# Where the joins, the softmax probabilities and each layer's last scoring stand in a graph network kernel

## What is computed

```python
def _gat_layer(x, src, dst, W_i, a_src_i, a_dst_i, b_i):
    h = (x @ W_i).reshape(n, H, C)
    es = jnp.einsum('nhc,hc->nh', h, a_src_i)
    ed = jnp.einsum('nhc,hc->nh', h, a_dst_i)
    e = es[src] + ed[dst]
    e = jnp.where(e > 0, e, NEG_SLOPE * e)
    m = jax.ops.segment_max(e, dst, num_segments=n)
    p = jnp.exp(e - m[dst])
    denom = jax.ops.segment_sum(p, dst, num_segments=n)
    alpha = p / denom[dst]
    msg = alpha[:, :, None] * h[src]
    out = jax.ops.segment_sum(msg, dst, num_segments=n)
    return out.reshape(n, H * C) + b_i
...
out1 = jax.ops.segment_sum(edge_attr, col, num_segments=n)
mx = jax.ops.segment_max(edge_attr, col, num_segments=n)
```

## Time and profile before

| | us |
|---|---|
| median of three runs | 9205.75 |
| lowest and highest of them | 9204.99 and 9205.83 |
| the profiled execution | 9206.7 |
| its span, first to last instruction | 9204.5 |

### The profile page before, as it was taken

How to read it: one execution, slowest core, us unless ns; L and a number is a source line. 1 busy time by engine, 2 the same in 40 slices (tenths; PEclk the granted TensorE clock), 3 DMA queues, 4 the chain that set the end, 5 groups by cost and what they waited for, 6 DMA issues and landing times.

```text
span 9204.5 us, 130223 instructions
## 1 busy us (share of the span) xinstructions
PE 5638.7 (61%) x34288; PEld 4521.8 (49%) x34288; DVE 5424.6 (59%) x12708; ACT 4487.3 (49%) x8146; POOL 5326.3 (58%) x5192
## 2 busy tenths in 40 slices
PE   4999879974555555555455555555534545455456
PEld 3777646653454544444445445444434444444444
DVE  6888721134666666666466666666645555555555
ACT  3555400024655555554455565555525555555554
POOL 2000100047777777775677777777757777777770
PEclk9999989965555555555555555555555555555558
DMA  3333335504444444443344444444423333333331
GB/s 102 136 140 140 126 140 188 181 9 124 113 123 116 118 121 114 124 113 89 88 120 116 123 113 122 117 116 122 103 66 80 84 82 86 80 86 81 86 80 32
DMA packets 601478, 989.12 MB, mean 107 GB/s; under 512 B 331106, under 2 KB 455043, under 8 KB 561523
## 3 DMA queue, kind: packets, MB, share of 16 engines
q0 software_dynamic: 163760, 357.05, 17.9%
q1 hardware_dynamic: 217540, 544.34, 16.9%
q10 hardware_dynamic: 219648, 81.82, 3.4%
HBM read 758.42 MB, written 224.34 MB: 107 GB/s over the span
## 4 chain that ended last, share of the span: by engine, by line
PE 27%; DVE 21%; DVEq 17%; POOL 16%; issue 13%; DMA 5%; ACT 1%; POOLq 0%; SPq 0%; ACTq 0%
POOL arena L650 14%; DVEq L1281 14%; PE bank L976 13%; DVE acc L1879 10%; DMA arena<-row_table,staged_idx 4%; PE bank L1199 3%; PE bank L1001 3%; DVE arena L1835 2%; PE bank L1139 2%; DVEq L1879 2%; DVE arena L1866 2%; DVE x_mem L1553 1%; DVE arena L1828 1%; PE bank L1264 1%; DVEq L1871 1%
## 5 line engine op out<-in xcount | busy, mean ns | idle before, releaser
L650 POOL DMA_INDIRECT arena<-row_table,staged_idx x4992 | 5039.4, 1009 | 1624.7 <-issue 1504.0
L1199 PE MATMUL bank<-arena 128*128 128x136 f32 x9984 | 2486.6, 429 | 1004.4 <-DVE acc L1879 843.5
L1199 PEld LDWEIGHTS bank<-arena 128*128 128x128 f32 x9984 | 2194.0, 315 | 1169.3 <-issue 1163.3
L1879 DVE TENSOR_TENSOR acc<-acc,bank 128x136 f32 x4992 | 1477.2, 296 | 1020.1 <-issue 796.5
L805 ACT ACTIVATE pick_dist<-col,dst_local 128x128 bf16<-128x128 f32 x4992 | 1518.5, 387 | 59.2 <-PE bank L1199 58.5
L976 PE MATMUL bank<-arena 128*128 128x385 bf16 (+1 forms) x7546 | 1342.2, 327 | 49.5 <-DVE arena L1657 33.0
L598 POOL TENSOR_TENSOR arena<-acc,node_stat 128x896 f32 x14 | 24.4, 1744 | 1729.1 <-POOLq L610 955.2
L1155 PE MATMUL bank<-ident,arena 128*32 128x128 f32 x624 | 161.5, 414 | 1347.3 <-DVE arena L1798 1347.3
L976 PEld LDWEIGHTS bank<-arena 128*128 128x128 bf16 x7546 | 711.1, 98 | 476.1 <-DVE arena L1657 33.2
L1795 DVE TENSOR_TENSOR arena<-arena 128x128 f32<-128x128 f32 x156 | 60.8, 390 | 1381.7 <-DMA arena<-row_table,staged_idx 1381.7
L1866 DVE TENSOR_TENSOR arena<-arena,prob 128x528 f32<-128x528 f32 x1248 | 837.3, 691 | 0.5
(11 more groups left out here) (356 smaller groups left out, 5676.2 us busy)
## 6 DMA issues: line engine op xcount, KB each, us to landing
arena<-dst_rows SPq DMA_DIRECT2D x156, 1024.0 KB, 5.8
cell_rows<-arena SPq DMA_DIRECT2D x76, 1568.0 KB, 5.2
arena<-cell_rows SPq DMA_DIRECT2D x76, 1568.0 KB, 6.5
arena<-row_table,staged_idx POOLq DMA_INDIRECT x4992
edge_stats<-x_mem ACTq DMA_DIRECT2D x416, 192.0 KB, 3.9
x_mem<-in_edge_attr SPq DMA_DIRECT2D x208, 192.0 KB
x_mem<-segment_flags SPq DMA_DIRECT2D x416, 96.0 KB
arena<-change_rows SPq DMA_DIRECT2D x312, 64.0 KB
```

What stands on the lines that cost most here:

```text
L650: pool.indirect_dma_start(gathered[:, at, :], None, table, bass.IndirectOffsetOnAxis(staged_idx[:, at:at + 1], 0)).then_inc(att_gathered[n ...
L1199: mm = pe.matmul(region(k)[:, 0:ROW], pick[:, k, :], gathered[:, b * GROUP + k, :], start=True, stop=True)
L1879: done = dve.tensor_tensor(row, row, region(m * BATCH + k), ALU.add)
```

## The change

Three things change.

1. In layer three alone (`n` of 2), `prob` is no longer the SBUF tensor but the first 128 columns of PSUM bank 0 or 1, by the group's parity (`prob_of`). ACT's exponential writes there, and `weigh` reads it from there.
2. `join_streams` is cut in two. `take_carry` (one copy out of bank 0) stays in front of layer three. The seven joins are written out and stand behind the adds of the groups 26 to 32 of that layer, one each; the first has the wait for the gathered statistics.
3. In group 50 of each layer (`head` and not `ahead`) the head of group 51 isn't woven in any more: DVE and PE do it behind all eight batches, ACT does its two exponentials behind its last picks (in layers one and two behind the copies of the statistics too).

```diff
+        JOIN_FROM = NG // 2
+        def prob_of(n, b):
+            if n < STATS_LAYERS:
+                return prob[:, b, :, :]
+            return bank[:, b, 0:HEADS * GROUP].rearrange("p (h s) -> p h s", h=HEADS)
...
-                    nc.scalar.activation(prob[:, b, :, :], score[:, :, :], ACT.Exp).then_inc(att.prob, 1)
+                    nc.scalar.activation(prob_of(n, b), score[:, :, :], ACT.Exp).then_inc(att.prob, 1)
...
-                            if head:
+                            if head and ahead:
                                 act_exps(n * NG + g + 1, 1 - b)
...
                     if n < STATS_LAYERS:
                         scan_out(n, g, 1)
+                    if head and not ahead:
+                        act_exps(n * NG + g + 1, 1 - b)
...
+                    between = head and ahead
                     for m in range(NBATCH):
                         sum_batch(G, b, m)
-                        if head and m == 2:
+                        if between and m == 2:
                             turn_scores(G + 1)
...
+                    if head and not between:
+                        turn_scores(G + 1)
+                        turn_ends(G + 1)
+                        turn_crossings(G + 1)
+                        turn_maxima(G + 1)
                     if head:
                         spread_scale(G + 1)
...
-            def join_streams():
+            def take_carry():
                 dve.wait_ge(st.carry_spread, 1)
                 dve.tensor_copy(carry_row[:, :], bank[:, 0, 0:2 * EA])
-                dve.wait_ge(n3.stats_gathered, 16 * NT)
-                then()
+                then()
+
+            def join_streams(i):
...
+                if i == 0:
+                    dve.wait_ge(n3.stats_gathered, 16 * NT)
+                    dve.sem_inc(dve_tick, 1)
...
-                                      prob[:, b, :, m * BATCH:(m + 1) * BATCH].rearrange("p h s -> p s h").unsqueeze(3)
+                                      prob_of(n, b)[:, :, m * BATCH:(m + 1) * BATCH].rearrange("p h s -> p s h").unsqueeze(3)
...
+                    if head and not between:
+                        score_edges(G + 1, 1 - b, use)
+                        first_scans(G + 1, 1 - b, use)
+                        carries(G + 1, 1 - b)
+                        last_scans(G + 1, 1 - b)
+                        shift_scores(G + 1, 1 - b, slot + GROUP)
+                    if n == STATS_LAYERS and JOIN_FROM <= g < JOIN_FROM + NTG:
+                        join_streams(g - JOIN_FROM)
 
                 if n == STATS_LAYERS:
-                    join_streams()
+                    take_carry()
                 score_edges(n * NG, 0, 0)
```

More of the change, by code:

```diff
@@ L1206, in pe_group @@
                     slot = it * (2 * GROUP) + (b + 2) * GROUP
+                    between = head and ahead
                     for m in range(NBATCH):
                         sum_batch(G, b, m)
-                        if head and m == 2:
+                        if between and m == 2:
                             turn_scores(G + 1)
-                        if head and m == 3:
+                        if between and m == 3:
                             turn_ends(G + 1)
-                        if head and m == 4:
+                        if between and m == 4:
                             turn_crossings(G + 1)
-                        if head and m == 5:
+                        if between and m == 5:
                             turn_maxima(G + 1)
@@ L1563, in keep_carry @@
                 done.then_inc(st.carried, 1)
[L1565 removed]
+            def take_carry():
                 dve.wait_ge(st.carry_spread, 1)
                 dve.tensor_copy(carry_row[:, :], bank[:, 0, 0:2 * EA])
[L1568 removed]
                 then()
+            def join_streams(i):
                 carry = [carry_row[:, m * EA:(m + 1) * EA].unsqueeze(1).to_broadcast([P, TG, EA]) for m in range(2)]
[L1571 to L1585 removed]
+                if i == 0:
+                    dve.wait_ge(n3.stats_gathered, 16 * NT)
+                    dve.sem_inc(dve_tick, 1)
+                rows = node_stats_in[:, i * TG:(i + 1) * TG, :]
+                mine, far = (on_bound[:, m, i * TG:(i + 1) * TG].unsqueeze(2).to_broadcast([P, TG, EA])
+                             for m in range(2))
+                dve.tensor_tensor(bound_part, carry[0], mine, ALU.mult)
+                then()
+                dve.tensor_tensor(rows[:, :, 0:EA], rows[:, :, 0:EA], bound_part, ALU.add)
+                then()
+                dve.tensor_tensor(bound_part, carry[1], mine, ALU.mult)
+                then()
+                dve.tensor_tensor(bound_part, bound_part, far, ALU.add)
+                then()
+                dve.tensor_tensor(rows[:, :, EA:2 * EA], rows[:, :, EA:2 * EA], bound_part, ALU.max
+                                  ).then_inc(st.joined, 1)
+                then()
             dve.tensor_copy(degree, acc_t[:, :, D]).then_inc(n1.degrees, 1)
@@ L1893, in dve_group @@
                         add_batch(G, slot, m)
-                        if head and m == 0:
+                        if between and m == 0:
                             score_edges(G + 1, 1 - b, use)
-                        if head and m == 1:
+                        if between and m == 1:
                             first_scans(G + 1, 1 - b, use)
-                        if head and m == 2:
+                        if between and m == 2:
                             carries(G + 1, 1 - b)
-                        if head and m == 3:
+                        if between and m == 3:
                             last_scans(G + 1, 1 - b)
-                        if head and m == 5:
+                        if between and m == 5:
                             shift_scores(G + 1, 1 - b, slot + GROUP)
```

14 lines of the change are left out of this document (removed).

## The result

The changed kernel takes 9171.67 us (median of six runs, 9169.31 to 9183.08), the kernel before, over all six of its runs, 9205.37. The ratio is 0.9966, with a 95% interval of 0.9956 to 0.9977: faster, by 33.7 us between the medians. The forecast was 28.3 us less, with 9167 to 9190 as its range. The profiled execution is the one of 9171.77 us; its span is 9170.0, 34.5 less than before.

The account below looks back on a forecast made before the run. POOL's stream of 4,992 gathers bounds the layers' bodies; at layer ends DVE, PE and ACT are the path. -8.3 + 0.6 - 20.6 = -28.3 us off the median 9205.75 gives 9177.4 us, range 9167 to 9190.

Parts of the forecast that it names:

- The rule of the held gather: A gather starting inside a DVE instruction with two SBUF operands begins its 0.94 us at that instruction's end, less 0.13 (scans 0.19).
- Part 1, 8.3 us less: Layer three: weighs reading probabilities from PSUM stop stretching gathers, 0.17 us a group over 49 groups; bounds 0 and 10.5.
- Only stretching after a group's last scan is returned: Layer three: gathers shortened earlier in a group run into the same scan; 41 gathers count, 8.5 us too long together.
- Part 2, +0.6 us: Joins moved behind adds of groups 26 to 32: 1.0 us regained at layer three's front, 1.6 of new stretching; bounds -1, +2.
- Part 3, 20.6 us less: Layer ends: seven batches run while group 51's rows are on the way; 5.9, 6.3 and 8.4 us less; bounds 17.5 and 21.5.
- Seven batches: Time of group 50's remaining batches at a layer's end, taken from group 51: 21.2 us in layer one, 16.7 in three.
- the hop: From the last head over PE and ACT to the rescale: matmul, ACT and gaps, some 1.2 us; bounds 0.9 and 2.2.
- (a): Layer three's weigh still stretches gathers with one SBUF operand; joins cost 1.3 net; 9186.4 us, chance 0.14.
- (d): Layer three's weigh keeps the port and gets longer by reading PSUM; 0.2 us more gives 9234 us; chance 0.03.
- (b): Last heads win nothing, as ACT's picks, scan-input loads or PE's queue delay the seven batches; 9198.0 us, chance 0.06.
- (e): Joins exceed their cover; POOL waits for PE's sums, 1 to 3 us in each of seven groups; about 9190, chance 0.04.
- (c): The weigh's length moves scans against POOL's 1.25 us raster, saving more in layer three; about 9165 us, chance 0.08.

Follow-up runs that it names:

- the two kernels with eight products: Changed kernel plus eight unread DVE products per group of layer three in idle time; both operands SBUF: 9192.87 us, one in PSUM: 9170.34 us.
- the two kernels that were to do it: Changed kernel; in layer three the second forward scan reads bank 3, or the first scan pair works through PSUM: 0.9980 and 0.9992 of before, on slower chips.

## Why the prediction was right, step by step

- **The bound.** Right. The gaps between gathers are unchanged (506.8 us in layer three before and after), and all that moved in a layer's body moved by the gathers' length. The sentence ahead of the prediction, that no engine is the bound as all are below 60%, is wrong for the layers (and PE has 61%): the share of busy time is over the whole span, and in the body of layer three POOL is busy for 76%, and the rest is nearly all `issue`.
- **The rule of the held gather.** Right for this change, and the two kernels with eight products show it by an operand's place alone. It isn't complete: the 106 gathers above are held by a weigh that starts after them.
- **Part 1, 8.3 us less.** The stream gave 9.0 with part 2 in it, which was put at +0.6. Step "Only stretching after a group's last scan is returned": in the sum it holds, 19.1 us taken from weighs, 10.4 taken back by scans. The first backward scan alone took 9.0 of the 10.4. No experiment isolates that step: the two kernels that were to do it ran where the gaps move. That the net is 9.0 and not 19 is measured. The weigh's length was taken as 0.70 unchanged; it fell by 7 ns, and for 20 ns the replay gave 10.5, so this may be the 0.7 us between 8.3 and 9.0; not tried.
- **Part 2, +0.6 us.** The front gave back 0.96 as said; the new place costs 0.88 in stretching, where 1.6 was taken. DVE's wait fell from about 11 to about 8 us, as said, and POOL waited no longer for PE's sums than before (1.2 us in layer three, 1.5 before). That the net is about zero follows from these rows as far as stretching goes; what the shift of DVE does to the scans can't be told from part 1's share.
- **Part 3, 20.6 us less.** The distance from the first batch to the rescale fell by 6.4, 6.6 and 9.0 us, 22.0 together, over the bound of 21.5. The head alone took 11.4 as taken. The step that was too careful is "Seven batches": 20.8, 21.0 and 16.2 us, where group 51's own rows gave 21.2 and 16.7, and the hop took 1.04 in place of 1.2. The bound let only the hop vary, so it came out too narrow. To the last add it is 22.4.
- **The sum.** 28.3 forecast, 31.4 in the stretches that the change touches, 34.5 in the profiled span. The 3.1 between these is not the change's, by the table above.
- **The rivals.** (a) and (d), the weigh that still holds: no stretched gather, a shorter weigh. (b), last heads that win nothing: DVE reaches the head with 0.18 us of idle time, behind batches without a gap. (e), a POOL that waits behind the joins: no gap over 0.4 us. (c), a raster that falls luckily: period 41.19 where the replay gave 41.23, so no.

## What to carry to other kernels

Where GpSimd issues the gathers and they are the bound, look at which DVE instructions read two SBUF operands: here one operand in PSUM took their hold off the gathers, at no cost in their own length. Remove the holds to the last one; here the scans that stood behind took back half of what the weighs gave. And work moved into a wait is worth at most the wait's length on the machine at hand: the same reordering gave 22 us where DVE waited 10 to 13 us at a layer's end, and cost 2.7 to 3.8 us at an end where it waited 1 us or not at all.

The kernel with none of the heads' scans on two SBUF operands, in any layer, is the fastest here, 9061.74 us, 1.5% under the one before and 1.2% under the changed one. In its layers one and two 97 and 98 us of stretching are left, by weighs and by the edge scans, which still have two SBUF operands.

## What the runs showed of the hardware

- A gather that starts inside a DVE product of 0.43 us with two SBUF operands is held as one inside a scan of 1.21 us is; with one of them in PSUM neither is (98 gathers by 19.1 us against none; 60 us of layer three against none). An exception: a gather that started inside a scan with a PSUM operand was stretched by the weigh with two SBUF operands right behind that scan, though this began 0.6 to 1.0 us after it (106 gathers, at most by 0.41 us).
- Of the same section of the Trainium skill another sentence agrees: two SBUF inputs contend with a GpSimd instruction that reads SBUF. A gather reads its 128 indices there (`staged_idx`); whether that access is the one that waits no run here tells.
- Chips differ by 12% on this kernel, 9199 to 9205 us on the ones of the first comparisons and 10339 to 10355 on the others, at the same 0.94 us a gather and the same DVE durations (an add 296 ns on both). The difference is engines that stand still, for a reason that is open. A term of 0.1% that was sized on one kind could not be seen on the other.
